# A graph network in two layers: GpSimd's wait for TensorE ahead of every second group of gathers

## The reference

```python
# layer 0
msg = edge_weight[:, None] * x[src]
agg = jax.ops.segment_sum(msg, dst, num_segments=N)
h = jax.nn.relu((x + agg) @ W1 + b1)
x = _layernorm(x + h @ W2 + b2)
# layer 1, with head = src, tail = dst, rel = edge_emb[edge_type]
for _ in range(3):                       # hops
    h, t = agg[head], agg[tail]
    att = jnp.sum((h @ q_w) * jnp.tanh(rel * t @ k_w), axis=1)
    w = softmax of att over the edges of one head
    agg = mean over the edges of one head of w[:, None] * rel * t, then scaled to norm 1
    out = out + agg + entity_emb
x = _layernorm(x + out)
```

## Time and profile before

| | us |
|---|---|
| runs shown: median (lowest to highest) | 12385.13 (12374.48 to 12412.58) |
| the profiled execution | 12507.17 |
| its span | 12505.4 |
| TensorE busy in the span | 8335.4 |
| GpSimd busy in the span | 6418.6 |
| gathers of the first layer: first to last start | 164.1 to 2783.6 |

### The profile page before, as it was taken

One profiled execution on the slowest core, in us unless ns is written; L12 is line 12 of the kernel. 1 busy time (PEld: TensorE's weight loads), 2 busy tenths in 40 slices (PEclk: granted clock), 3 DMA queues, 4 the chain that ended last, 5 costly groups with the idle time before them and its releaser, 6 DMA issues. The chain is left out here.

```text
span 12505.4 us, 247136 instructions
## 1 busy us (share of the span) xinstructions
PE 8335.4 (67%) x47197; PEld 6405.1 (51%) x47197; DVE 6238.6 (50%) x27880; ACT 6039.9 (48%) x15796; POOL 6418.6 (51%) x6756
## 2 busy tenths in 40 slices
PE   2466666665877777787766666666665666666665
PEld 2344444444555555555545555455554555555554
DVE  3566666666444444444444444444444444444445
ACT  1266666664444444444444444444444455444444
POOL 4666666652444444444435555555554555555553
PEclk7567767777888888888878888988888888888887
DMA  2111111121444444444444444444444444444444
GB/s 68 44 42 43 43 43 42 43 39 43 150 147 147 147 147 148 147 147 147 146 126 130 129 131 130 129 127 129 128 130 112 132 131 131 130 133 130 131 131 110
DMA packets 1390851, 1403.19 MB, mean 112 GB/s; under 512 B 239511, under 2 KB 1066680, under 8 KB 1390136
## 3 DMA queue, kind: packets, MB, share of 16 engines
q1 hardware_dynamic: 1173398, 951.42, 24.5%
q0 software_dynamic: 216064, 444.28, 14.6%
q10 hardware_dynamic: 876, 2.56, 0.1%
HBM read 888.87 MB, written 183.76 MB: 86 GB/s over the span
## 5 line engine op out<-in xcount | busy, mean ns | idle before, releaser
L622 POOL DMA_INDIRECT tails<-node_rows,idx x4992 | 4730.1, 948 | 4631.0 <-PE banks L1844 2470.4
L1849 PE MATMUL banks<-rt,weight_t 128*128 128x129 f32 x9984 | 1714.0, 324 | 2055.9 <-DVE acc L1764 1794.9
L1857 ACT ACTIVATE weight_t<-banks 128x512 f32<-128x512 f32 x1248 | 745.5, 597 | 4354.0 <-remote 2559.4
L1764 DVE SCALAR_TENSOR_TENSOR acc<-acc,fade,banks 128x129 f32 x4992 | 1723.4, 345 | 2023.9 <-issue 920.2
L1849 PEld LDWEIGHTS banks<-rt,weight_t 128*128 128x128 f32 x9984 | 1483.7, 227 | 2291.2 <-issue 1956.8
L1770 DVE CUSTOM_DVE_ANT_0 att<-banks,mask 128x128 f32<-128x128 f32 x4992 | 1242.7, 287 | 1923.7 <-remote 1771.1
L622 POOL DMA_INDIRECT l_rows<-in_x_dram,l_idx x1664 | 1591.9, 957 | 1053.0 <-issue 453.9
L1829 PE MATMUL banks<-right,window 128*128 128x128 f32 x9984 | 1782.3, 336 | 16.6 <-issue 16.5
L1829 PEld LDWEIGHTS banks<-right,window 128*128 128x128 f32 x9984 | 1620.7, 246 | 56.7 <-issue 19.9
L1877 ACT ACTIVATE weight<-att,low 128x128 f32<-128x128 f32 x4992 | 1589.1, 397 | 18.0 <-DVE low L1800 9.2
L1840 PE MATMUL banks<-rtt,k_sb 128*128 128x512 f32 x2496 | 1451.7, 667 | 1.4 <-ACT rtt L1864 1.4
(11 more groups left out here) (309 smaller groups left out, 9689.6 us busy)
## 6 DMA issues: line engine op xcount, KB each, us to landing
window<-qt SPq DMA_DIRECT2D x4992, 64.0 KB
rel<-rel_kept SPq DMA_DIRECT2D x832, 256.0 KB
rows_in<-tile_rows SPq DMA_DIRECT2D x416, 256.0 KB
rel_kept<-rel SPq DMA_DIRECT2D x416, 256.0 KB
mask<-mask_kept SPq DMA_DIRECT2D x832, 128.0 KB
tails<-node_rows,idx POOLq DMA_INDIRECT x4992
mask_kept<-mask SPq DMA_DIRECT2D x416, 128.0 KB
l_rows<-in_x_dram,l_idx POOLq DMA_INDIRECT x1664
```

The lines of the kernel that those rows point to most:

```text
L622: e.indirect_dma_start(out=rows[:, g, t, :], out_offset=None, in_=of, in_offset=bass.IndirectOffsetOnAxis(ap=idx[:, b, first + t:first + t ...
L1764: e.scalar_tensor_tensor(to, to, fade[:, g2, t:t + 1], bank[b_acc + t // 2][:, t % 2 * WIDE:t % 2 * WIDE + WIDE], ALU.mult, ALU.add).then_ ...
L1849: mm = e.matmul(bank[b_acc + t // 2][:, t % 2 * WIDE:t % 2 * WIDE + WIDE], weight_t[:, s.slot(4, 2), t, :], rt[:, s.slot(4, UNROLL), t, :] ...
```

## The change

`pool_rows` gets an argument `per`, 1 by default. The wait for `s_step` stands only ahead of groups whose number is a multiple of `per`, and its register is counted up by `per` there. The first layer's call passes 2; the hops' call is as it was. The waits for the free slot and the row numbers are as they were.

```diff
-        def pool_rows(e, name, rows, idx, of, s_free, s_step, behind):
+        def pool_rows(e, name, rows, idx, of, s_free, s_step, behind, per=1):
...
-                if g > behind:
+                if g > behind and g % per == 0:
                     e.wait_ge(s_step.h, s_step.at(g - behind))
                 gather(g)
...
-                    e.wait_ge(s_step.h, stepped)
+                    if g % per == 0:
+                        e.wait_ge(s_step.h, stepped)
                     gather(g)
                     e.reg_add(freed, freed, 1)
-                    e.reg_add(stepped, stepped, 1)
+                    if g % per == 0:
+                        e.reg_add(stepped, stepped, per)
...
-                    pool_rows(e, "l0", rows, idx, x, s_rt, s_acc, 5)
+                    pool_rows(e, "l0", rows, idx, x, s_rt, s_acc, 5, 2)
```

## The result

The kernel after took 12528.07 us (median of four runs, 12511.43 to 12536.12) beside 12385.74 us for the kernel before in the same runs (12374.48 to 12412.58). The ratio is 1.0108, 95% interval 1.0095 to 1.0120. That is 142 us slower, where 32 us faster was forecast, and it lies outside the range.

What follows compares the result with a forecast made beforehand. No engine was taken as full: GpSimd's bursts and pauses, holding TensorE's updates, set the loop's pace. Terms 0 - 32 + 0 + 0 + 0 = -32 us took 12385 to 12353, rounded 12355 us; range 12260 to 12450.

Steps and rivals of the forecast that it cites:

- The bound: First-layer gather loop: no engine full; GpSimd's bursts and pauses set the pace, 6.36 us a group, holding TensorE's updates.
- B: Rival: TensorE is late by itself and GpSimd only follows, so nothing moves, 12385 us; 20% together with D.
- Instructions taken away: GpSimd's loop body: four of eight groups lose a wait and a register addition, hidden; 0, bound -120 us.
- The wait taken away ahead of odd groups: Steady loop, 352 groups: bursts of one become twos at 12.31 us; -32 us, bounds 169 less to 218 more.
- No other wait takes its place: Odd groups in the gather loop: row numbers and free slot are already ready, so no other wait holds them.
- The first 64 groups: Loop's light start: bursts of three become twos and fours at equal cost; 0, or 10 us if all twos.
- The bound of +218 us: Steady loop's slow side: four-group bursts wait one more 4.46 us compute step, 6.98 us a group over 352 groups.
- rival A: Rival: four-group bursts after even groups hold TensorE's sums back, 3.3 us each; +67 us with 30, 12452; 18%.
- The hops: Layers after the first: call unchanged, GpSimd code only lies some instructions earlier; 0, with 10 us to each side.
- The same rhythm should hold in the runs: Profiled execution, 12507.17 us, is 122 us above the runs' median, 1.0%; its loop rhythm was taken to hold there.
- C: Rival: four-group bursts and compute keeps up, 5.88 us a group, -169 us, 12216; 12%.
- D: Rival: the edit does not bite because odd groups rarely waited, within 10 us; 20% together with B.

Runs made afterwards that it cites:

- single gather: Kernel before, but only the first of each group's four first-layer gathers issued, other tiles left zero: 11751.31 us, ratio 0.9385.
- memsets: Kernel before, with three of each group's four first-layer gathers replaced by GpSimd memsets, each waited for: 11869.89 us, ratio 0.9588 on a slower chip.
- every fourth group: Changed kernel with per = 4, waiting for TensorE's sum only ahead of every fourth group: 12997.30 us, ratio 1.0489 to before on a slower chip.
- looser wait: Kernel before with all waits and additions kept, but odd groups ask for one sum less: 12654.44 us, ratio 1.0103.
- lead of four: Changed kernel, its wait ahead of even groups asking for the sum of four groups back instead of five: 12622.47 us, ratio 1.0085 to before.
- lead of six: Kernel before, every group waiting for the sum of six groups back instead of five: 12519.50 us, ratio 1.0003.
- half groups: Kernel before plus a GpSimd wait in mid-group for VectorE's half of the sums six groups back: 12569.92 us, ratio 1.0147 on a slower chip.

## Why the prediction was wrong

**The bound: right in kind.** It was said that no engine is full, that the rhythm of bursts and pauses sets the pace, and that updates of TensorE are held by GpSimd's burst. The single gather (6.31 to 4.47 us for a group), the memsets (0.9588) and every fourth group (1.0489) show on this kind of chip that compute is late because of trains of gathers. That it is TensorE's updates alone is not so: VectorE's own sequence has gaps in a burst too. B, TensorE late by itself, falls: it would have left the change at 1.

**Instructions taken away, 0: right.** With all of them kept the loss is the same, 1.0103 against 1.0108, so they are worth nothing that shows.

**The wait taken away ahead of odd groups, -32 us: this step failed.** As the prediction put it, 133.5 bursts of two at 12.31 us replace ones and twos, at 2.5 us of pause each. The count was right: 127 pauses for 255.5 groups. The length was wrong: 3.43 us in the mean, and 13.34 us for a burst of two. The forecast of 24 us less for 267 groups meant a pace of 6.36 - 0.09 = 6.27 us for a group; at 6.65, over 352 groups, that is off by 134 us, and from -32 to the loop's +106 are 138. The 12.31 us came from bursts of two in the kernel before, and these were a selection. There, GpSimd ran two groups together only when enough sums had come through; where only one had, it sent one group, 6.65 us, and this was the cheap way to wait for the next. The change shuts that way. Then the even group waits for the held sum and for one whole step after it, which makes the 32 pauses of over 4 us (9.77 us in the example), and the pauses rise from 384.4 / 267 = 1.44 us for a group to 435.9 / 255.5 = 1.71. The loop's 106 us are (6.65 - 6.36) x 352 = 102 us in the steady part and a rest ahead of it. The make-up of before, 47 ones and 110 twos, was worked out from two totals; the trace has 42 ones, 104 twos and 5 threes, with means of 6.82, 12.53 and 19.38 us. Even with 12.53 a gain would have been forecast, so this is not what failed.

**"No other wait takes its place": right by the program.** The profile puts 14 pauses, 49.2 us, to the free slot (`l_weighed` in the list), but as said above that wait cannot be the last one there.

**The first 64 groups, 0: right within the 10 us given.** 132 gathers against 134 in 200 us is 1.5% of that stretch, 3 us, for a part that is some 380 us long 6 us. As was said, bursts became twos and fours there, three of them of four groups from 390 to 560 us.

**The bound of +218 us**, which was worked out as one more step of 4.46 us before GpSimd may go on, is the mechanism that came true, in bursts of two instead of four. The prediction applied it to bursts of four alone, as a bound and in the price of rival A, and took a burst of two as safe, because 110 of 157 bursts were twos already.

**The hops, 0: in the experiments right.** On the chip with 12511 us the loop's last gather and the runs move together, by 145 and 143 us for the looser wait, by 107 and 111 for the lead of four, by 764 and 760 for the single gather (for the lead of six, by -10 and +8). For the changed kernel itself the loop grew by 106 us and the runs by 142. The likely reason for the 36 us between is that its chip is not that of the profile of before: the kernels on a chip with 12384 us end their gathers at 3352.0 (every fourth, +614 us in the runs) and 2929.0 (half groups, +186), which puts that of before at some 2740 there, and 2886.5 - 142 gives 2744. The kernel with memsets on that chip does not fit as well: 2259.8, -514 us in the runs, gives 2774. This is worked out, not shown, and the cause of the 36 us stays open: no profile of the kernel before on such a chip was taken.

**"The same rhythm should hold in the runs", though the profiled execution stood 122 us above them: careless.** The sign of the effect survives, but 1.0% of difference between a profile and its runs was a warning that they might not come from the same chip.

**Rival A** was the right rival with the wrong place and price. It asked for fewer than 110 pauses with a mean over 4 us, and "remote" waits of `apart` above 384.8 us. It came out at 127 pauses of 3.43 us, and 216.8 us for `apart`, with 173.1 us now put down to TensorE's matmul beside them; the two together, 389.9 us, were 384.8 + 63.4 before. So that sign was no good: the same waiter's idle time moved from one label to the other. The pace, 6.65, was its sign that came true. Its place did not: five bursts of four in the stretch, 26.3 us each or 6.6 for a group, are neither many nor dearer than the rest. C and D fall: the pace is above 6.0 and the number of pauses did change.

On one kind of chip the waiters for TensorE stood in "remote" waits of up to 9.8 us in the kernel before, with one gather and three memsets in none. The Trainium skill, page "Trainium Architecture — The Big Picture", section "What this means for kernel authors", says that on the engines' side of SBUF only the port pair of VectorE and GpSimd contends. That is about access to SBUF and says nothing of semaphore updates or of issuing, so the prediction's "the sum would be 0" did not follow from it, and the late updates here do not contradict it. The Trainium skill, page "Perfetto Trace Analysis", section "Tensor Engine Instruction (MATMUL, LD_WEIGHTS)", says that a matmul's end is estimated and its semaphore is pushed after PSUM's acknowledgement; that leaves room for a late update, and no run here shows which part of this path is slow.

## What to carry to other kernels

A duration read from bursts that the kernel chose to make does not hold for bursts that it is forced to make: ask what the cases left out did instead, and price the wait for the second event from the first one's delivery. A fine-grained wait can be worth keeping though it stops an engine more often: here it let a single group out on the first late sum, where the coarse one waited a whole step for the second. Before trusting a gain or loss of 1%, compare the profiled execution with the runs, and measure on more than one chip: this change costs 1.1% on one (142 of 12386 us) and nothing on another (0.9999).

## What the runs showed of the hardware

- The same kernel takes 12384 and 12511 us on two of the chips met and 9115, 9121 and 9128 on three others, 36% more, with the same 944 ns for a gather. No chip was met twice, so this can be a state of a chip as well as the chip. Most of the difference lies behind this loop: 6871 us follow the last gather of the changed kernel on the faster chip (9129.1 - 2258.4), 9645 on the slower. The mean granted clock of the changed kernel is 0.804 on one of the first kind and 0.907 on one of the second, with TensorE busy 8358.5 and 7142.9 us. Which of the two is cause stays open. In this loop the clock goes with the pace: at 5.04 us for a group the slower chip grants 0.79 (memsets, 900 to 2200 us), and at 5.05 the faster one 0.78. In the changed kernel's loop the engines other than TensorE are busy as long for a group on both (VectorE 1081.70 / 255.5 = 4.23 us and 4.19, which is 1078.77 us in a stretch of 1300 us with 1029 gathers).
- On the slower chips updates of TensorE that fall late into a train of gathers are seen only when it has ended: in the examples 1.4 us after its end with eight gathers, 3.2 us with sixteen, where a waiter had stood for 17 us. VectorE's own instructions come late in a train too (194.8 us of "issue" in 1300 us, 7.7 on the faster chip). Three memsets in place of three gathers take both away. Whether the descriptors or the transfers do it, and whether they delay the updates or the issuing of instructions, was not tried.
